# Attention in a transformer block on one core: the maximum pass split into three row-group matmuls and one full-height matmul

## What is computed

```python
def _L0_attn_ref(x, Uq, Vq, bq, Uk, Vk, bk, Uv, Vv, bv):
    B, S, D, H, R = (8, 256, 256, 8, 32)
    DH = D // H
    b_, s_, _ = x.shape                       # 8, 2048, 256
    xh = x.reshape(b_, s_, H, DH)
    q = _lowrank(xh, Uq, Vq, bq)
    k = _lowrank(xh, Uk, Vk, bk)
    v = _lowrank(xh, Uv, Vv, bv)
    scores = jnp.einsum('bqhd,bkhd->bhqk', q, k) / DH ** 0.5
    attn = jax.nn.softmax(scores, axis=-1)
    out = jnp.einsum('bhqk,bkhd->bqhd', attn, v)
    return out.reshape(b_, s_, D)
```

## Time and profile before

| what | value |
|---|---|
| median of three runs | 4940.31 us |
| the profiled execution, its own time | 4941.97 us |
| span of the profiled execution | 4940.2 us |
| PE busy | 3962.8 us (80%) |
| VectorE (DVE) busy | 3256.7 us (66%) |
| ScalarE (ACT) busy | 2839.3 us (57%) |
| GpSimd (POOL) busy | 2797.0 us (57%) |
| mean granted clock of TensorE | 0.933 |

### The profile page before, as it was taken

One profiled execution on the slowest core, in us unless ns is written; L12 is line 12 of the kernel. 1 busy time (PEld: TensorE's weight loads), 2 busy tenths in 40 slices (PEclk: granted clock), 3 DMA queues, 4 the chain that ended last, 5 costly groups with the idle time before them and its releaser, 6 DMA issues. The chain is left out here.

```text
span 4940.2 us, 69035 instructions
## 1 busy us (share of the span) xinstructions
PE 3962.8 (80%) x21362; PEld 1555.6 (31%) x21362; DVE 3256.7 (66%) x3736; ACT 2839.3 (57%) x5625; POOL 2797.0 (57%) x966
## 2 busy tenths in 40 slices
PE   0156476499999999999999999999999999930166
PEld 0134354133333333333333333333333333310144
DVE  8744365577767767776776776677677777549644
ACT  4143355266666666666666666666666666634043
POOL 0011000277777777777777777777777777753111
PEclk9999788699999999999999999999999999965599
DMA  6200499556676675766667575676657666467200
GB/s 222 76 29 5 149 353 328 113 124 139 131 157 134 136 154 110 158 127 144 146 132 151 108 163 122 138 157 128 144 119 162 129 138 129 92 192 246 78 5 5
DMA packets 316558, 676.10 MB, mean 137 GB/s; under 512 B 24780, under 2 KB 208608, under 8 KB 268832
## 3 DMA queue, kind: packets, MB, share of 16 engines
q0 software_dynamic: 48000, 340.81, 34.0%
q1 hardware_dynamic: 234624, 297.04, 20.9%
q10 hardware_dynamic: 33568, 33.69, 2.0%
HBM read 198.90 MB, written 136.48 MB: 68 GB/s over the span
## 5 line engine op out<-in xcount | busy, mean ns | idle before, releaser
L1462 DVE TENSOR_REDUCE at_part_max<-at_ps_max 128x4 f32<-128x2048 f32 x1024 | 2347.7, 2293 | 1022.6 <-PE at_ps_max L1589 1021.6
L1561 ACT ACTIVATE at_probs<-at_ps_s 128x512 f32<-128x512 f32 x4096 | 2233.4, 596 | 1045.3 <-PE at_ps_s L1658 989.8
L1442 POOL TENSOR_TENSOR at_pool_sum<-at_pool_sum,at_probs 128x2048 f32<-128x2048 f32 x448 | 2055.7, 4589 | 289.9 <-DMA at_probs<-at_probs 277.3
L1658 PE MATMUL at_ps_s<-at_qs,at_ks 97*128 97x512 f32 (+1 forms) x4096 | 1715.8, 472 | 72.0 <-ACT at_probs L1561 36.3
L1658 PEld LDWEIGHTS at_ps_s<-at_qs,at_ks 97*128 97x128 f32 (+1 forms) x4096 | 683.0, 188 | 1496.9 <-ACT at_probs L1561 1208.1
L1622 PE MATMUL at_ps_acc<-at_probs,at_v 128*32 128x512 f32 x8192 | 1098.0, 608 | 0.9 <-ACT at_probs L1561 0.9
L1589 PE MATMUL at_ps_max<-at_ks,at_qs 32*128 32x512 f32 x4096 | 525.2, 501 | 89.8 <-DVE at_part_max L1462 43.3
L1419 POOL DMA_DIRECT2D at_probs<-at_probs x320 | 282.0, 881 | 494.8 <-PE at_ps_acc L1622 465.9
L1442 POOL TENSOR_TENSOR at_pool_sum<-at_probs 128x2048 f32<-128x2048 f32 x64 | 292.2, 4566 | 98.7 <-ACT at_probs L1561 98.7
L1589 PEld LDWEIGHTS at_ps_max<-at_ks,at_qs 32*128 32x128 f32 x4096 | 198.1, 183 | 444.0 <-DVE at_part_max L1462 296.6
L238 PE MATMUL s_pt<-s_ident,s_sall 128*128 128x128 f32 x2 | 0.9, 447 | 359.5 <-DVE s_sall L205 359.5
(11 more groups left out here) (198 smaller groups left out, 2505.4 us busy)
## 6 DMA issues: line engine op xcount, KB each, us to landing
at_probs<-at_probs POOLq DMA_DIRECT2D x320, 1024.0 KB, 7.3
qk_parts<-pr_hi SPq DMA_DIRECT2D x32, 1024.0 KB, 6.5
qk_parts<-pr_lo SPq DMA_DIRECT2D x32, 1024.0 KB, 6.2
at_qs<-qk_parts SPq DMA_DIRECT2D x320, 64.0 KB, 1.9
at_ks<-qk_parts SPq DMA_DIRECT2D x80, 256.0 KB
s_x<-in_x SPq DMA_DIRECT2D x16, 1024.0 KB, 7.4
after_ffn<-s_y ACTq DMA_DIRECT2D x16, 1024.0 KB, 8.2
pr_x<-after_ffn SPq DMA_DIRECT2D x8, 2048.0 KB, 12.5
```

Of the source, the lines that this page charges most:

```text
L1442: nc.gpsimd.tensor_tensor(acc, a, probs[:, c % RING], ALU.add).then_inc(pool_added, 1)
L1462: nc.vector.reduce_max(part_max[:, :, t, c], ps_max[:], AX.X).then_inc(part_max_done, 1)
L1561: nc.scalar.activation(probs[:, c % RING, h], ps_s[:, j % 2], ACT.Exp, scale=SCALE).then_inc(exp_done, 1)
L1658: nc.tensor.matmul(ps_s[:, j % 2], ks[rows, g, h, c * P:(c + 1) * P], qs[rows, un % NQB, h, :], start=True, stop=True).then_inc(scores, 1)
```

## The change

The fourth head (index 3) leaves the row-group pass. Its max matmul now takes all 96 rows of the stacked parts (the exact score, one full-height matmul, `last_head_for_max`); the other three stay in three row groups of 32 (`three_heads_for_max`). VectorE reduces the one bank with one instruction and the three banks with a second one, each with semaphores of its own (`last_max_scores`, `last_part_max_done` beside the two that were there). All four heads now have the same layout, high parts of heads 2 and 3 in rows 64 to 95, the row of maxima in row 96: the memsets go, loads per q are 7 for 8, the row of maxima is one transfer for two, `qs` and `ks` have 97 rows for 128. And PE's order within a cycle is another: the last head's max matmul right behind the second score matmul (S1), then the transposes if any, then the three heads, then S2 and S3, and PV with `close_z` at the end. ScalarE's `copy_acc` comes after the fourth exponential of cycle 0 for the second.

```diff
-    HI_AT = (0, DH, 2 * DH, 3 * DH)
-    SHIFT_AT = (3 * DH, 3 * DH, 3 * DH, 2 * DH)
-    LAST_ROW = (3 * DH + 1, 3 * DH + 1, 3 * DH + 1, 4 * DH)
-    HI_ROWS = ((0, 0, 1), (DH, 1, 2), (2 * DH, 2, 3), (3 * DH, 3, 4))
+    STACK = 3 * DH
+    HI_AT = (0, DH, 2 * DH)
+    HI_ROWS = ((0, 0, 1), (DH, 1, 2), (2 * DH, 2, 4))
...
-    LOADS = 8 * 16
+    LOADS = 7 * 16
...
-                for first, end in ((0, HG - 1), (HG - 1, HG)):
-                    to = SHIFT_AT[first]
-                    sp.dma_start(qs[to:to + 1, un % NQB, first:end].bitcast(F32)
-                                 .rearrange("a h (t q) -> a (h t) q", q=P),
-                                 max_row[first * QT:end * QT].bitcast(F32)).then_inc(max_in, 16)
+                sp.dma_start(qs[STACK:STACK + 1, un % NQB].bitcast(F32).rearrange("a h (t q) -> a (h t) q", q=P),
+                             max_row[:].bitcast(F32)).then_inc(max_in, 16)
...
-            nc.vector.memset(ks[odd_one, :, HG - 1].bitcast(F32), 0.0).then_inc(zero_rows, 1)
-            nc.vector.memset(qs[odd_one, :, HG - 1].bitcast(F32), 0.0).then_inc(zero_rows, 1)
...
+                dve.wait_ge(last_max_scores, unit * FOURS + n + 1)
+                nc.vector.reduce_max(part_max[:, HG - 1, t, c:c + 1], ps_max[:, HG - 1], AX.X
+                                     ).then_inc(last_part_max_done, 1)
                 dve.wait_ge(max_scores, unit * FOURS + n + 1)
-                nc.vector.reduce_max(part_max[:, :, t, c], ps_max[:], AX.X).then_inc(part_max_done, 1)
+                nc.vector.reduce_max(part_max[:, 0:HG - 1, t, c], ps_max[:, 0:HG - 1], AX.X
+                                     ).then_inc(part_max_done, 1)
...
-                        if carry and j == 1:
+                        if carry and j == PER_CYC - 1:
                             copy_acc(unit)
...
-            def scores_for_max(unit, un, n, first_unit=False):
+            def last_head_for_max(unit, un, n, first_unit=False):
 
                 t, c = divmod(n, QT)
                 if n >= 1 or not first_unit:
 
+                    pe.wait_ge(last_part_max_done, unit * FOURS + n)
+                h = HG - 1
+                nc.tensor.matmul(ps_max[:, h], qs[0:STACK, un % NQB, h, t * P:(t + 1) * P],
+                                 ks[0:STACK, un % BU // NU, h, c * 512:(c + 1) * 512], start=True, stop=True
+                                 ).then_inc(last_max_scores, 1)
+
+            def three_heads_for_max(unit, un, n, first_unit=False):
+
+                t, c = divmod(n, QT)
+                if n >= 1 or not first_unit:
+
                     pe.wait_ge(part_max_done, unit * FOURS + n)
-                for h in range(HG):
+                for h in range(HG - 1):
                     rows = slice(HI_AT[h], HI_AT[h] + DH)
...
+                        for_max(last_head_for_max, i)
+                        if carry and i == TURN_Z_IN:
+                            turn_z(unit)
+                        if carry and i == TURN_O_IN:
+                            turn_o(unit)
+                        for_max(three_heads_for_max, i)
+                        if turning:
+                            pe.wait_ge(max_row_done, unit + 2)
+                            score(j + 1)
+                        for n in range(2, PER_CYC):
+
+                            pe.wait_ge(exp_done, unit * TILES + j + n - 1)
+                            score(j + n)
                         if i > 0:
                             pv(unit, un, i - 1)
                         elif carry:
                             pv(unit - 1, (un - 1) % BU, NC - 1)
                         if carry and i == CLOSE_Z_IN:
                             close_z(unit - 1, un - 1)
-                        if turning:
-                            pe.wait_ge(max_row_done, unit + 2)
-                            score(j + 1)
-                        for n in range(2, PER_CYC):
-
-                            pe.wait_ge(exp_done, unit * TILES + j + n - 1)
-                            score(j + n)
-                        if carry and i == TURN_Z_IN:
-                            turn_z(unit)
-                        if carry and i == TURN_O_IN:
-                            turn_o(unit)
-                        max_four(i)
```

More of the change, by code:

```diff
@@ L1260, in sem @@
             return handle
-        qs = sb("qs", [P, NQB, HG, UQ], F32R)
-        ks = sb("ks", [P, NG, HG, S], F32R)
+        qs = sb("qs", [STACK + 1, NQB, HG, UQ], F32R)
+        ks = sb("ks", [STACK + 1, NG, HG, S], F32R)
         v = sb("v", [P, NG, NC, P])
@@ L1282, in attend @@
         ones_row = sem("ones_row")
-        zero_rows = sem("zero_rows")
         q_in = [sem(f"q_in{n}") for n in range(NQB)]
@@ L1288, in attend @@
         max_scores = sem("max_scores")
+        last_max_scores = sem("last_max_scores")
+        last_part_max_done = sem("last_part_max_done")
         part_max_done = sem("part_max_done")
@@ L1404, in _ @@
             pool.wait_ge(consts, 2)
[L1405 to L1408, removed]
+            nc.gpsimd.memset(ks[STACK:STACK + 1].bitcast(F32), 1.0).then_inc(ones_row, 1)
             def batch(b, first_batch=False):
@@ L1450, in _ @@
         def _(dve):
-            odd_one = slice(SHIFT_AT[HG - 1], SHIFT_AT[HG - 1] + DH)
-            nc.vector.memset(ks[odd_one, :, HG - 1].bitcast(F32), 0.0).then_inc(zero_rows, 1)
-            nc.vector.memset(qs[odd_one, :, HG - 1].bitcast(F32), 0.0).then_inc(zero_rows, 1)
             def part_max_of(unit, n, first_unit=False):
@@ L1460, in part_max_of @@
                 t, c = divmod(n, QT)
+                dve.wait_ge(last_max_scores, unit * FOURS + n + 1)
+                nc.vector.reduce_max(part_max[:, HG - 1, t, c:c + 1], ps_max[:, HG - 1], AX.X
+                                     ).then_inc(last_part_max_done, 1)
                 dve.wait_ge(max_scores, unit * FOURS + n + 1)
-                nc.vector.reduce_max(part_max[:, :, t, c], ps_max[:], AX.X).then_inc(part_max_done, 1)
+                nc.vector.reduce_max(part_max[:, 0:HG - 1, t, c], ps_max[:, 0:HG - 1], AX.X
+                                     ).then_inc(part_max_done, 1)
                 if n == FOURS - 1:
+                    dve.wait_ge(last_part_max_done, unit * FOURS + FOURS)
                     dve.wait_ge(part_max_done, unit * FOURS + FOURS)
@@ L1520, in row_of_max @@
                 if not first_unit:
-                    act.wait_ge(max_in, unit * 32)
+                    act.wait_ge(max_in, unit * 16)
                 nc.scalar.copy(max_row[:], ps_s[0:HG * QT, bank, 0:P]).then_inc(max_row_done, 1)
@@ L1600, in _ @@
             for n in range(FOURS):
-                scores_for_max(0, 0, n, first_unit=True)
+                last_head_for_max(0, 0, n, first_unit=True)
+                three_heads_for_max(0, 0, n, first_unit=True)
             pe.wait_ge(q_in[1], LOADS)
@@ L1604, in _ @@
             for n in range(MAX_LEAD):
-                scores_for_max(1, 1, n)
-            pe.wait_ge(ones_row, 2)
+                last_head_for_max(1, 1, n)
+                three_heads_for_max(1, 1, n)
+            pe.wait_ge(ones_row, 1)
             def batch(b, first_batch=False, last=False):
@@ L1656, in score, with for_max @@
                         c, h = divmod(j, HG)
-                        rows = slice(0, LAST_ROW[h])
+                        rows = slice(0, STACK + 1)
                         nc.tensor.matmul(ps_s[:, j % 2], ks[rows, g, h, c * P:(c + 1) * P], qs[rows, un % NQB, h, :],
                                          start=True, stop=True).then_inc(scores, 1)
-                    def max_four(n):
+                    def for_max(step, n):
                         ahead = un + 1 + (n + MAX_LEAD) // FOURS
@@ L1666, in max_four @@
                             return
-                        if n == 0:
+                        if n == 0 and step is last_head_for_max:
                             pe.wait_ge(q_in[ahead % NQB], (b * (BU // NQB) + ahead // NQB + 1) * LOADS)
@@ L1670, in max_four @@
                                 pe.wait_ge(k_in[ahead // NU % NG], (b + ahead // BU + 1) * LOADS)
-                        scores_for_max(unit + ahead - un, ahead, n)
+                        step(unit + ahead - un, ahead, n)
                     if u == 0:
                         pe.wait_ge(v_in[g], b * 16 + 16)
-                    pe.wait_ge(max_in, unit * 32 + 32)
+                    pe.wait_ge(max_in, unit * 16 + 16)
                     for i in range(NCYC):
```

## The result

The change takes 5020.95 us (median of four runs, 5017.92 to 5023.80) against 4940.81: the ratio estimated from the runs is 1.0154, 95% interval 1.0143 to 1.0166 (the quotient of the two medians is 1.0162, inside it). It is slower by 80 us, where +40 was forecast.

A forecast was written before the change was run, and what follows sets the result against it. A loop through two ScalarE exponentials, a score matmul and PV was taken to bound the kernel, not VectorE. Net 48 − 11 + 3 = +40 us gave 4980 us, 0.8% slower; range 4942 to 5040.

The forecast's parts named there:

- What bounds: Attention cycle: a ScalarE loop of 3.08 us sets the 3.10 us pace; the PE-VectorE ping-pong, 2.90, has 0.2 to spare.
- The split: VectorE's two reductions: 0.69 us for one bank, 1.76 for three, together 2.45 in a cycle of 3.1, so no bound.
- One more matmul: The added full-height max matmul after S1 costs PE 0.23 us, its weight load covered; upper bound 0.42.
- the dear last head: Rival, chance 0.10: the last head's weight load lies open, 0.42 us for 0.23, adding 88 us: 5068.
- Cycle by cycle: Old against new cycle lengths within a unit: +0.78 us a unit, +48 us for the 62 units between first and last.
- First pass: Opening 20 steps, a real PE-VectorE ping-pong at 1.2 GHz: 3.20 us a step falls to 2.67, −11 us.
- Slow clock ... +3: Some ten cycles after the start and batch ends, bound by PE at 1.2 GHz: +0.3 us each, +3.

The follow-up runs named there:

- e5: The kernel before the change, with VectorE's maximum reducing only 256 of the 512 columns of each bank; 4921.2 us, ratio 0.9959.
- e7: The kernel before the change, with each exponential over 256 of 512 columns; 4858.2 us in one run.
- e3: The change, with ScalarE's ring-slot waits moved from a chunk's first exponential to the last exponential of the chunk ahead; 5008.5 us, ratio 1.0137.
- e6: The kernel before the change, with ScalarE's ring-slot waits moved in front of the third exponential of the chunk ahead; 4955.9 us, ratio 1.0031.
- e1: The change's split kept at the place of the old max matmuls, PE's old order otherwise; 4965.3 us, ratio 1.0052.
- e2: The change's order on PE, with the earlier kernel's max matmuls (four row groups, one reduction over four banks); 5013.3 us, ratio 1.0142.

## Why the prediction was right in kind and short in size

- *What bounds*: right. The loop of two exponentials and PV is shown by e5 (less VectorE work, same cycle), e7 (shorter exponentials, 2.90) and the pair e3 and e6. The summary's 1022.6 us of idle VectorE pointed at a wait with 0.2 us to spare.
- *The split*: 691 and 1750 ns for 0.69 and 1.76 forecast. *One more matmul*: 0.23, its load covered. So the rival of the dear last head falls, at every cycle.
- *Cycle by cycle*: +0.88 a unit for +0.78. Cycle 13 (+0.20 for +0.17), cycle 6 (+0.03 for 0) and cycle 8 (+0.07 for +0.05) make up most of the difference; cycle 1 rose by 0.09, unforecast, and cycle 0 fell by as much. 48 us forecast, about 55 over all 62 units.
- *First pass*: −10.6 for −11. The granted clock stayed at 0.50, 1.2 GHz, there.
- *The step that failed* is "Cycle by cycle", in that it took the exponential after S0 to start 0.54 after it in every batch, from a row on S2. In the first and last batch it is 0.62. Their 15 units cost +26.7, of which 15 x 0.88 = 13 is the common part: some 14 us, nearly all of which e3 gives back (12.4).
- *"Slow clock ... +3"* was mis-sized: what stands at the batch ends is a stop for code, and it grew. Ten units cost +25.2, of which 8.8 is the common part: 16 for 3.

48 − 11 + 3 = 40 forecast; 55 − 10.6 + 14 + 16 = 74 by these terms, 75.6 between the spans.

The measured 5021 lies above the 4960 to 5005 that the prediction gave by the bounds of its own terms. It lies inside the range of 4942 to 5040 only because that range took in the lower part of the dear last head, a rival that did not come true. That the range held is thus in part luck: about 30 us of the loss come from two places that no term or rival priced.

## What to carry to other kernels

Before a wait is removed, add up the loop it belongs to, from the producer's start to the producer's next start, and compare it with the cycle: an engine that idles because its own loop is shorter than the cycle gains nothing by being fed sooner. Reordering such a program turns the loop onto other instructions, so check what stands ahead of those, in every copy of the code: waits that were free may not be. A place with nothing else to do, such as the first pass here, is where the split pays.

## What the runs showed of the hardware that I had not expected

- An exponential behind several waits starts 0.08 us later where its loop is written out (0.62 for 0.54), 38 ns of it a semaphore instruction.
- The branch back of the loop over batches takes PE 3.4 to 4.5 us in one order of its work (before, e1) and 5.8 to 7.6 in the other (the change, e2), and after it PE runs for some microseconds at 1.2 GHz (granted clock 0.50 from 1808 to 1812 in the change).
- VectorE is recorded as starting the next instruction before the last has ended: in the change the one-bank reduction is recorded from 2440.79 to 2441.48, the three banks from 2441.40.
